# Windowed attention kernel: scores two pairs ahead, values two behind, and the two work banks used in turn

## The reference

```
x = x + conv_experts(_gn(x))      # shared 1x1 + two chosen experts, group norm and silu each
xn = _gn(x)
q, k, v = qkv_w @ xn + qkv_b      # per 8x8 window: 64 tokens, 8 heads of 16
attn = softmax(q k^T / 4 + bias)
out = attn v + depthwise7x7(v)
x = x + proj_w @ out + proj_b
```

## Time and profile before

| | |
|---|---|
| median of 3 runs | 931.99 us (929.11 to 934.04) |
| the profiled execution | 934.59 us |
| its span, first to last instruction | 932.9 us |
| TensorE busy | 743.6 us (80%) |
| VectorE busy | 578.1 us (62%) |
| ScalarE busy | 457.7 us (49%) |
| GpSimd busy | 197.0 us (21%) |
| mean granted TensorE clock | 0.879 of 2.4 GHz |
| setup and first images, up to the query projection of image 1 | 141.8 us |
| from there to the query projection of image 14, 13 periods | 595.8 us |
| depthwise convolution and end, from 818 us | 115 us |

### The profile page before, as it was taken

The page is one execution under the profiler, slowest core; times in us unless marked ns, Lnnn a source line. Parts: engine busy times, 40 slices in busy tenths (PEclk is TensorE's granted clock), DMA queues, the critical chain, the costliest instruction groups (busy, mean ns, idle before and its releaser), DMA issues.

```text
span 932.9 us, 18414 instructions
## 1 busy us (share of the span) xinstructions
PE 743.6 (80%) x6926; PEld 422.7 (45%) x6926; DVE 578.1 (62%) x1136; ACT 457.7 (49%) x746; POOL 197.0 (21%) x289
## 2 busy tenths in 40 slices
PE   6143768888888989888989887979797989978785
PEld 5121334454545554545454545454545456534321
DVE  4724456675767666767676757575757587632296
ACT  1204546555555564646464646464646465344422
POOL 3122123131213140403130313131313020000044
PEclk9976969797979797979888988888988989999999
DMA  9224444545464545455554545454546254586435
GB/s 353 106 71 116 139 113 146 145 128 156 144 178 136 163 148 150 150 153 165 142 170 128 173 136 173 123 173 120 177 132 177 67 176 132 161 276 217 156 157 203
DMA packets 84046, 145.29 MB, mean 156 GB/s; under 512 B 24179, under 2 KB 48886, under 8 KB 83958
## 3 DMA queue, kind: packets, MB, share of 16 engines
q1 hardware_dynamic: 58102, 100.89, 34.8%
q0 software_dynamic: 21248, 25.36, 10.9%
q10 hardware_dynamic: 4608, 17.86, 5.2%
HBM read 84.21 MB, written 51.41 MB: 145 GB/s over the span
## 4 chain that ended last, share of the span: by engine, by line
PE 41%; DMA 19%; DVE 16%; ACT 8%; issue 7%; SPq 6%; POOL 1%; POOLq 1%; ACTq 0%; DVEq 0%
PE g L1061 11%; DMA sk_d<-khl 10%; PE g L1057 5%; PE g L1079 4%; PE t L1127 4%; DMA stack<-sk_d 3%; SPq L298 3%; ACT xw L540 3%; PE s L1116 3%; PE pv L1142 3%; DMA vt<-x 3%; PE t L1241 2%; PE s L1112 2%; SPq L292 2%; PE s L1241 2%
## 5 line engine op out<-in xcount | busy, mean ns | idle before, releaser
L806 DVE BATCH_NORM_STATS2 st<-y 128x6 f32<-128x512 f32 x96 | 66.6, 694 | 147.6 <-ACT y L522 147.6
L522 ACT ACTIVATE y<-g 128x512 f32<-128x512 f32 x96 | 57.2, 596 | 167.0 <-PE g L1061 87.0
L1061 PE MATMUL g<-xsh,wsel 96*128 96x512 f32 x256 | 127.8, 627 | 14.0 <-DMA xsh<-xs 10.5
L595 ACT ACTIVATE pt<-t 128x512 f32<-128x512 f32 x128 | 76.2, 597 | 118.8 <-PE t L1127 112.2
L870 DVE TENSOR_REDUCE mx<-s 128x8 f32<-128x512 f32 x128 | 87.8, 686 | 69.6 <-PE s L1116 69.6
L1127 PE MATMUL t<-ident,less 128*128 128x128 f32 x512 | 97.6, 321 | 3.7 <-DVE less L874 3.7
L1142 PE MATMUL pv<-vp,pt 128*64 128x34 f32 x2048 | 95.2, 242 | 5.0 <-ACT pt L595 4.8
L1112 PE MATMUL s<-bias,ident 128*128 128x512 f16 x128 | 56.7, 443 | 52.9 <-DMA stack<-sk_d 52.8
L1142 PEld LDWEIGHTS pv<-vp,pt 128*64 128x64 f32 x2048 | 80.1, 154 | 31.4 <-issue 25.0
L874 DVE TENSOR_TENSOR less<-s,mx 128x512 f32<-128x512 f32 x128 | 88.5, 692 | 4.4
L1079 PE MATMUL g<-xw,w 128*128 128x512 f32 x128 | 66.7, 640 | 15.4 <-ACT y L522 11.7
(11 more groups left out here) (159 smaller groups left out, 1158.5 us busy)
## 6 DMA issues: line engine op xcount, KB each, us to landing
xsh<-xs POOLq DMA_DIRECT2D x64, 210.0 KB, 5.4
stack<-sq_d SPq DMA_DIRECT2D x96, 128.0 KB, 3.1
stack<-sk_d SPq DMA_DIRECT2D x192, 64.0 KB, 2.8
xs<-xn ACTq DMA_DIRECT2D x16, 578.0 KB, 2.9
vt<-x SPq DMA_DIRECT2D x4, 2048.0 KB, 17.7
xin<-x POOLq DMA_DIRECT2D x16, 512.0 KB, 5.8
acc_d<-xr SPq DMA_DIRECT2D x16, 512.0 KB, 5.5
sq_d<-qhl SPq DMA_DIRECT2D x16, 512.0 KB, 7.7
```

Of the source, the lines that this page charges most:

```text
L522: act.activation(y[:, k, h * HALF:(h + 1) * HALF], g[h][:, :], ACT.Identity).then_inc(g_free[h], 1)
L595: act.activation(pt[:, p % 2].rearrange("p i w n -> p (i w n)"), tbk[p % 2][:, :], ACT.Exp).then_inc(sem["exp_done"], 1)
L806: last = v.bn_stats(st[:, 2 * k + h, :], y[:, k, h * HALF:(h + 1) * HALF])
L1061: last = mm(g[h][:, :], wsel[:, k - 1, C * dy:C * dy + C], xsh[:, k - 1, dy + 16 * h:dy + 16 * h + 16, 0:W], start=(dy == 0), stop=(dy == 1))
```

## The change

- **Lag.** In pair step p TensorE runs turn p first, then scores p+2 (before: scores p+1, then turn p), then values p-2 (before p-1). `pt` has three buffers and exp p waits for values p-3. `maxima` and `outputs` move along.
- **Banks.** There is one list of uses; the n-th use has bank n mod 2, whatever its half. Halves of q, y1, y2 and pr become uses of their own and alternate with other work.
- **Places.** y2 halves and q halves of the next image go to steps 0 and 1, k to 2, v to 3, vt to 4, y0 (now of b+3) and pr half 0 to 5, y1 half 0 and pr half 1 to 6, y1 half 1 and ot half 0 to 7. The silus go to step 3 behind v_out and turn_out, the window (now of b+2) to step 7.
- **Keys.** q and k are saved by halves, with a semaphore for each; stacking is split into `stack_q` and `stack_k`. place_v, load_x1, save_xr and save_acc take other places on SyncE's queue; the taps are loaded after the loop.

The core of the diff:

```diff
...
+        if 0 <= j < B:
+            order.extend((name, j, h) for h in halves)
...
+        use("y2", b + 2, (0,))
+        use("q", b + 1, (0,))
+        use("y2", b + 2, (1,))
+        use("q", b + 1, (1,))
+        use("k", b + 1)
+        use("v", b + 1)
+        use("ot", b - 1, (1,))
+        use("vt", b + 1)
+        use("y0", b + 3)
+        use("pr", b - 1, (0,))
+        use("y1", b + 3, (0,))
+        use("pr", b - 1, (1,))
+        use("y1", b + 3, (1,))
+        use("ot", b, (0,))
     for b in range(B):
         use("last", b)
-    return tuple({key: n for n, key in enumerate(half)} for half in order)
+    return {key: (n % 2, n // 2) for n, key in enumerate(order)}
...
+            def save_half(j, half, name, dst, src, saved):
+
+                cols = slice(HALF * half, HALF * half + HALF)
+                wait_emptied(sp, name, j, half)
+                if j:
+                    sp.wait_ge(stacked[half], STACK * j)
+                sp.dma_start(dst.rearrange("t c n -> c t n")[:, :, cols], src[:, :, cols]).then_inc(saved[half], 16)
...
                 if has1:
                     save_q(b + 1)
                     save_k(b + 1)
+                    stack_q(b + 1, 0)
+                    stack_k(b + 1, 0)
+                if b:
+                    load_x1(b - 1)
+                if has1:
+                    stack_q(b + 1, 1)
+                    stack_k(b + 1, 1)
+                    place_v(b + 1)
+                if has2:
+                    save_xr(b + 2)
                 if b:
                     save_acc(b - 1)
             save_xr(0)
             save_q(0)
             save_k(0)
+            for half in range(2):
+                stack_q(0, half)
+                stack_k(0, half)
+            place_v(0)
             save_xr(1)
             images(step)
+            for c in range(TAP_RING):
+                load_taps(c)
+            load_x1(B - 1)
             save_acc(B - 1)
...
+                if has2:
+                    rsqrt(b + 2, 0, 3)
                 if has3:
                     load_rows(b + 3)
-                if has2:
+                if b + 4 < B:
+                    load_x(b + 4)
                 if has3:
                     choose_affine(b + 3)
                 if has1:
                     split_v(b + 1)
+                if has2:
+                    rsqrt(b + 2, 1, 1)
...
-                    act.wait_ge(sem["pv_done"], s - 1)
-                act.activation(pt[:, p % 2].rearrange("p i w n -> p (i w n)"), tbk[p % 2][:, :],
+                if s > 2:
+                    act.wait_ge(sem["pv_done"], s - 2)
+                act.activation(pt[:, s % 3].rearrange("p i w n -> p (i w n)"), tbk[p % 2][:, :],
                                ACT.Exp).then_inc(sem["exp_done"], 1)
             def step(b, has1, has2, has3):
...
+                    if p < 2:
                         if has2:
+                            copy_y(b + 2, 2, (p,))
                         if has1:
+                            high_qk(b + 1, 0, p)
+                        if has3 and p == 0:
+                            normalise(b + 3)
+                    if p == 2 and has1:
+                        high_qk(b + 1, 1, 0)
+                        high_qk(b + 1, 1, 1)
+                    if p == 3:
+                        if has1:
+                            v_out(b + 1)
                         if b:
                             turn_out(b - 1, 1)
                         if has2:
+                            for k in range(3):
+                                silu(b + 2, k)
+                    if p == 4 and has1:
+                        vt_out(b + 1)
+                    if p == 5 and has3:
+                        copy_y(b + 3, 0)
+                    if p == 6 and has3:
+                        copy_y(b + 3, 1, (0,))
+                    if p == 7:
+                        if has2:
+                            window(b + 2)
                         if has3:
+                            copy_y(b + 3, 1, (1,))
                         turn_out(b, 0)
...
+                    if has2 and p == 3:
                         group_variance(b + 2, 0, 3)
+                    if has2 and p == 7:
+                        group_variance(b + 2, 1, 1)
+                    if has1 or p < PAIRS - 2:
+                        maxima(b + (p + 2) // PAIRS, (p + 2) % PAIRS)
+                    if p == 1 and b:
+                        outputs(b - 1, ROWS - 1)
+                    elif p % 2 and p > 1:
+                        outputs(b, p // 2 - 1)
+                    if p < 2:
+                        if has2:
+                            y_stats(b + 2, 2, (p,))
                         if has1:
+                            low_qk(b + 1, 0, p)
+                    if p == 2 and has1:
+                        low_qk(b + 1, 1, 0)
+                        low_qk(b + 1, 1, 1)
+                    if p == 3 and has2:
                         y_coefs(b + 2)
+                    if p == 4:
                         if has1:
                             turn_v(b + 1)
                         if has2:
                             residual(b + 2, 0)
+                    if p == 5:
+                        if has2:
+                            residual(b + 2, 1)
+                            residual(b + 2, 2)
+                    if p == 6:
+                        if has3:
+                            y_stats(b + 3, 0)
+                        if b:
+                            add_projection(b - 1, 0)
+                    if p == 7:
+                        if has2:
+                            x_coefs(b + 2)
+                        if has3:
+                            y_stats(b + 3, 1)
+                        if b:
+                            add_projection(b - 1, 1)
...
             def step(b, has1, has2, has3):
                 for p in range(PAIRS):
                     turn_scores(b, p)
+                    if has1 or p < PAIRS - 2:
+                        scores(b + (p + 2) // PAIRS, (p + 2) % PAIRS)
+                    if p > 1:
+                        values(b, p - 2)
                     elif b:
+                        values(b - 1, p + PAIRS - 2)
+                    if p < 2:
+                        if has2:
+                            convolve(b + 2, 2, (p,))
                         if has1:
+                            project_qk(b + 1, 0, p)
+                    if p == 2:
+                        if has1:
+                            project_qk(b + 1, 1, 0)
+                            project_qk(b + 1, 1, 1)
                         if has2:
+                            average(b + 2, 0, 3, AV16)
+                    if p == 3:
+                        if has1:
+                            project_v(b + 1)
                         if b:
                             turn_outputs(b - 1, 1)
+                    if p == 4 and has1:
+                        project_vt(b + 1)
+                    if p == 5:
+                        if has3:
+                            convolve(b + 3, 0)
+                        if b:
+                            project_outputs(b - 1, 0)
+                    if p == 6:
+                        if has3:
+                            convolve(b + 3, 1, (0,))
+                        if b:
+                            project_outputs(b - 1, 1)
                         if has2:
+                            average(b + 2, 1, 1, AV4)
+                    if p == 7:
+                        if has3:
+                            convolve(b + 3, 1, (1,))
                         turn_outputs(b, 0)
...
```

407 lines of the change are left out of this document (151 added, 256 removed).

## The result

The changed kernel takes 972.5 us, the median of four runs (965.5 to 976.2), beside 931.8 for the kernel before: 1.043 times as long, 95% interval 1.036 to 1.049. The forecast was 979, with a range of 938 to 1012. The profiled execution took 976.2 us, with a span of 974.1; it stands 3.7 above the median, so distances are taken between spans (932.9 before).

A forecast was written before the change was run, and what follows sets the result against it. TensorE's pace, 45.83 us an image, with its idle time and the half clock behind it, was taken as the bound; 44.0 + 3.0 + 2.3 gave 49.3 a period, with +1.4 for the ends 979 us, range 938 to 1012.

The forecast's parts named there:

- Keys: First scores of an image: the stack is there at 10.5 to 14.2 us, scores at 17.9; the 3.5 us stall goes.
- TensorE's work: TensorE's own work stays the same: 1.83 us a pair, some 34.7 us an image at full clock.
- Step 5: Shared convolution waits 3.4 us for the bank that vt_out frees, behind the silus and exp on ScalarE.
- Step 6: Second output projection, ready at 3.65 us, waits until 4.65 for add_projection to free its bank; the step takes 5.7.
- Step 7: Transposes of ot wait 3.85 us for add_projection, behind window, copy and y1's statistics; the step takes 8.05.
- The rows: load_rows of b+3 on GpSimd, behind rsqrt in step 3, is in time: rows used in step 6, over 15 us later.
- The clock: TensorE at half clock behind the stalls of steps 7 and 5: 3.0 and 2.3 us a period in the sum.
- The ends: Outside the periods: first query 2.5 us earlier, image 0's step 3 shorter, tail 6.9 longer; together +1.4 us.
- One spell an image (1): Only one half-clock spell an image on TensorE: period 46.3 to 47.5, 940 to 955 us; chance 0.16.
- TensorE as the bound (3): Chains have unseen slack and TensorE bounds: 35 to 37 us a period, 795 to 820 us; chance 0.05.
- the late keys (4): Split key path late by shared DMA engines: two to four us more a period, 1005 to 1030 us; chance 0.05.
- the stop ahead of table changes (5): ScalarE stops 1.28 us ahead of each of two table changes: period 51.9, 1012 us; chance 0.02.

The follow-up runs named there:

- reordered: Changed kernel with both output projections in step 4, vt in 5, y0 in 6, y1 halves in 7, x1 loaded at step start: 857.3 us, 0.920 of before.
- before_turn_first: The kernel before, with each pair's turn ahead of the next pair's scores, same lag: 925.3 us, 0.993 of the kernel before.
- add_early: Changed kernel with add_projection's second half ahead of y1's statistics on VectorE in step 7: 895.1 us, 0.959 of the kernel before.
- both_early: Changed kernel with add_projection's second half ahead of y1's statistics and the rows of b+3 issued ahead of the first rsqrt: 878.9 us.
- both_identity: both_early with the three silus run as plain scale and bias, without their table loads: 888.4 us, 0.955 of the kernel before.
- keys_first: reordered with queries and keys projected in steps 0 and 1 and the third convolution behind them in step 2: 862.6 us.
- keep_busy_rows: Changed kernel with rows issued ahead of rsqrt, plus unread TensorE matmuls ahead of the shared convolution and step 7's transposes: 913.1 us.

## Why the prediction was right, point by point

*Keys.* Right that no scores wait for the stack, but partly by luck: both terms were mis-sized. The half save took 2.2 us where I took the middle of 3.8 and 7.5, below both my ends. I had halved a duration that was due to the rows beside it. And for "the nine issues and their arrival" I took "at most the 6.2 us" of the kernel before. SyncE's key issues in the changed kernel:

```profile
344.10 4.04 SPq L296 DMA_DIRECT2D stack<-sk_d  x6
```

and TensorE's wait for them in reordered:

```profile
363.45 0.61 PE L1123 MATMUL s<-bias,ident 128*128 128x512 f16 x1 [4.54 <-DMA stack<-sk_d]
```

In the changed kernel the nine issues begin at 342.58, and the last of them, at 347.4, lands 10.2 us later, at 357.6: 15.0 us in all, and 0.8 ahead of the scores at 358.41. In five other images from 290 to 550 us it was 8.7 to 14.9 us. So the keys owe it to the other stalls that they were in time. Without these, in reordered, the stack took 14.9 us again (348.53 to 363.45) and the scores waited for it, so the cover named ("at 13.3 if nothing else stalled it") wasn't there.

*TensorE's work.* The pair's 1.83 was a mis-sized term: 1.57 in the changed kernel (340.51 to 342.08), 1.53 in before_turn_first. I had taken the price in one order for another. Eight pairs make 2.1 us an image less.

*Step 5.* Right in place and order. It waits 4.17 us, not 3.4: of that 0.8 us, three cheaper pairs ahead of it give 0.8.

*Step 6.* The 1.0 us for add_projection shows only where rows are early; once in 250 to 650 us otherwise.

*Step 7.* 3.97 us against 3.85, and add_early shows that the order on VectorE makes it.

*The rows.* Wrong. "Its rows are used in step 6, over 15 us later" took a distance for an all-clear. It is 15 us from the first issue (344.61) and 11 from the end of the last, which landed after 14. I had not priced their landing beside 18 stack issues. The waits of the changed kernel from 250 to 650 us, in the columns of both_early:

```profile
PE g L1073 <- ACT vp L577: 33.3, 8, 4.2
PE g L1170 <- DVE x L914: 31.7, 8, 4.0
PE g L1077 <- DMA xsh<-xs: 16.2, 7, 3.3
```

In 400 us, 8.0 full periods, that is 10.2 us an image, where the steps above had 9.2.

*The clock.* Right in kind. With 34.7 less 2.1 of work and 10.2 of waits, 42.8 us, the full period of 49.74 leaves 6.9 for half clock; I had 5.3. This is a remainder, not a measurement. The granted clock of the full periods was 0.84, some 16 us an image at half clock; half of that, 8, is the most that it can cost. In the image shown the spells last 3.4 us behind step 5 (I had 4.6), 3.4 behind the rows (I had none) and 10.2 behind step 7 (I had 6 to 8, and put only 3.0 us for it in the sum).

*The ends.* Mis-sized: the sum had +1.4 us. Beside thirteen full periods the first query came 5.8 us earlier (I had 2.5), image 0's step was 4.3 shorter (3), the tail 4.0 longer (6.9; the late taps show as the wait of 7.65 us at 862.71), and the depthwise stage, which I had left alone, 3.5 shorter, at a mean clock of 0.96 instead of 0.94. Together -9.6 against my +1.4. The thirteen periods give +50.8 against my 45.1; of that difference of 0.44 a period the cheaper pairs are -2.1, the missed rows and longer stop +1.0, half clock +1.6. So that the total came so near (46.5 us forecast, 41.2 measured between spans) was in part luck: terms of both signs cancelled.

*The rivals.* One spell an image (1) fell by the windows, 2.4 GHz throughout (2) too; TensorE as the bound (3) by every wait; the late keys (4) don't show in the changed kernel, where they were 0.8 us from it in the image above, and do in both_identity and reordered; the stop ahead of table changes (5) by both_identity.

What stays open: what the lag of two and the banks by use are each worth, since no run has one without the other; how the time of a save or a row load splits between shared DMA engines and the order in their queues, and why the keys of both_identity were later than in both_early.

## What to carry to other kernels

Where banks alternate by use, each piece of work waits for the engine that empties the bank two uses before: ask what that engine does first, and put the instruction that frees a bank ahead of one that waits for a third engine. Two instructions that changed places were worth 77 us here; the whole change around them, with that done, was worth 37.

A transfer's duration belongs to its place: a time read in the old place, as the 6.2 us for the stack here, doesn't carry over to the new one. Before moving a prefetch, list what moves beside it in its new place and what waits for that. And when a stall is removed, the next one is often just as long and was hidden under it: price the second and third before counting the gain.

## What the runs showed of the hardware

- Turn, scores, values cost 1.53 to 1.57 us a pair; scores, turn, values 1.83, with the same instructions.
- A 512 KB store of the keys lands in 3.1 us where little else moves and 7.6 beside row loads; 256 KB in 2.2 and in 7.1 to 8.7. Halving bought under a microsecond, the place up to six.
- TensorE's clock fell to 1.2 GHz also where no wait was long: in keys_first none of the waits from 250 to 650 us is over 2.8 us, and it was at half clock for 163 us in all. In one image the clock fell at 402 us, behind waits of 0.86 and 0.91 us.
- One microsecond less at half clock was worth 0.27 to 0.31 us in keep_busy_rows.
- A table load cost 1.28 us, with no more than 0.02 us between it and the instructions on either side.
- From the first of nine stack issues to the landing of the last it took 15.0 us in one image of the changed kernel, where an image of the kernel before had 6.2.
